# Projections of Q, K and V as three products of rounded parts; a descriptor ring of half the size, at most three scatters under way, and x normalised behind them

## What is computed

```python
x = x + xattn(layernorm(x), ctx)          # 16 heads of 16
x = x + ffn(layernorm(x))                 # 8 experts, the best 2 per token

def xattn(x_q, x_kv):
    q = split_heads(x_q @ wq.T + bq)
    k = split_heads(x_kv @ wk.T + bk)
    v = split_heads(x_kv @ wv.T + bv)
    attn = softmax(q @ k.T / 4)
    return merge_heads(attn @ v) @ wo.T + bo

def ffn(x):
    gates = top 2 of softmax((x @ Wg + bg) / 5), made to sum to 1
    return sum over experts e of gates[e] * (gelu(x @ W1[e] + b1[e]) @ W2[e] + b2[e])
```

## Time and profile before

| | us |
|---|---|
| runs: median of 3 (lowest to highest) | 797.72 (795.2 to 801.35) |
| the profiled execution's own time | 804.22 |
| its span, first to last instruction | 802.5 |
| TensorE busy | 754.3 |
| VectorE busy | 610.5 |
| ScalarE busy | 455.4 |
| GpSimd busy | 393.8 |
| attention part, from 41 (first transposed scores) to about 525 | 484 |
| tail | about 275 |

### The profile page before, as it was taken

The page is one execution under the profiler, slowest core; times in us unless marked ns, Lnnn a source line. Parts: engine busy times, 40 slices in busy tenths (PEclk is TensorE's granted clock), DMA queues, the critical chain, the costliest instruction groups (busy, mean ns, idle before and its releaser), DMA issues.

```text
span 802.5 us, 16338 instructions
## 1 busy us (share of the span) xinstructions
PE 754.3 (94%) x4672; PEld 451.0 (56%) x4672; DVE 610.5 (76%) x1127; ACT 455.4 (57%) x663; POOL 393.8 (49%) x357
## 2 busy tenths in 40 slices
PE   9999999999999999999999897869999999999995
PEld 4443344444444444444444333349999888988994
DVE  6787678798797788788788787657777887676774
ACT  2066676776766766766676674944345434443441
POOL 6506143647637728728725613306643564444444
PEclk9999999999999999999999999999999999999998
DMA  7765767657666766657658467767554465354441
GB/s 225 208 180 174 211 180 214 215 185 246 206 194 231 215 195 242 193 188 247 188 172 270 148 175 264 257 241 164 92 101 75 82 144 101 64 80 70 69 75 12
DMA packets 90660, 136.24 MB, mean 170 GB/s; under 512 B 15456, under 2 KB 49216, under 8 KB 90192
## 3 DMA queue, kind: packets, MB, share of 16 engines
q1 hardware_dynamic: 76592, 117.33, 48.4%
q0 software_dynamic: 13296, 17.09, 12.2%
q10 hardware_dynamic: 688, 0.79, 0.3%
...
## 4 chain that ended last, share of the span: by engine, by line
PE 68%; DMA 10%; issue 6%; DVE 5%; ACT 5%; SPq 4%; POOLq 1%; another core or an unknown queue 0%; POOL 0%; DVEq 0%
PE ps_pv L1576 13%; PE ring L1563 10%; PE ring L1742 8%; PE ring L1724 7%; PE ring L1550 7%; PE ps_x L1607 7%; DMA out<-y_sb,xs 7%; PE ps_x L1627 4%; ACT probs L1045 3%; PE ps_x L1617 3%; DMA den<-oT 3%; PE ring L1733 2%; DVE negm L1117 2%; PE ps_x L1637 2%; PE ps_x L1594 1%
## 5 line engine op out<-in xcount | busy, mean ns | idle before, releaser
L1117 DVE TENSOR_REDUCE negm<-ring 128x2 f32<-128x1024 f32 x256 | 310.0, 1222 | 74.3 <-PE ring L1550 63.2
L1045 ACT ACTIVATE probs<-ring 128x1024 f32<-128x1024 f32 x256 | 260.1, 1024 | 90.4 <-PE ring L1563 72.0
L926 POOL DMA_INDIRECT out<-y_sb,xs x70 | 108.8, 1554 | 152.7 <-DMA out<-y_sb,xs 81.0
L1576 PE MATMUL ps_pv<-probs,v_aug 128*32 128x512 f32 x1024 | 136.4, 605 | 3.8 <-ACT probs L1045 3.5
L1563 PE MATMUL ring<-kq 64*128 64x512 f32 x512 | 125.0, 489 | 8.1 <-DVE negm L1117 7.0
L1550 PE MATMUL ring<-kq 64*128 64x512 f32 x512 | 106.2, 413 | 9.5 <-ACT probs L1045 5.7
L1563 PEld LDWEIGHTS ring<-kq 64*128 64x128 f32 x512 | 47.3, 183 | 108.8 <-issue 73.3
L1078 ACT CAST xsT_hi<-ps_pv 128x256 fp32r<-128x256 f32 x70 | 26.1, 373 | 132.8 <-PE ps_pv L1715 120.3
L1742 PE MATMUL ring<-w_hi,hT_hi 128*128 x284 | 85.3, 300 | 0.8 <-DMA w_hi<-w_dram 0.8
L819 POOL DMA_INDIRECT xs_dram<-xg,rows x64 | 63.2, 987 | 39.5 <-issue 15.7
L1742 PE MATMUL ring<-w_lo,hT_hi 128*128 x284 | 80.2, 282 | 0.0
...
## 6 DMA issues: line engine op xcount, KB each, us to landing
...
```

The lines of the kernel that those rows point to most:

```text
L926: pool.indirect_dma_start(out=out, out_offset=bass.IndirectOffsetOnAxis(ap=xs[j % AHEAD][:, TOKEN:TOKEN + 1].bitcast(I32), axis=0), in_=re ...
L1045: nc.scalar.activation(probs[kt][:, 2 * jp:2 * jp + 2, :], ring[PLACE["ST", u, p] % RINGS][:], ACT.Exp).then_inc(exp_done, 1)
L1117: nc.vector.tensor_reduce(negm[:, v % 2, :, jp, kt], ring[PLACE["MX", v, p] % RINGS][:], AX.X, ALU.max, negate=True).then_inc(max_free, 1)
L1576: mm = nc.tensor.matmul(ps_pv[2 * DH * j:2 * DH * (j + 1), :], v_aug[:, kt, HPG * g + j, :], probs[kt][:, j, :], start=(kt == 0), stop=(kt ...
```

## The change

From batch 1 on the projections are made of three float32r products in place of one float32 product. For this the weights are split once, in the prologue: ScalarE makes `wk_hi`, `wq_hi`, `wv_hi` (128x512 each), GpSimd the low parts (`low_weights`). The context is split for each batch: ScalarE makes `kv_hi` in two halves (`high_kv`, slots (3, 3) and (3, 4)), GpSimd `kv_lo` (`low_kv`, 128x1024). Of the transposed x ScalarE makes the high part, where it made a plain copy before, and VectorE the low part (`low_x`, 128x512, slots (2, 7) and (3, 2)); `ps_x` is free only after the low part. XT0 moves from slot (2, 7) to (2, 6). The second staging of an expert's weights on ScalarE moves from (3, 2) to (3, 5).

The low parts lie where the whole values lay, and `xn_hi` where `xn` lay. So there is one `kvT` in place of two, its load waits for V1 of the batch before and stands after `fetch_o(i, 0)` and `load_w1(i)` in SyncE's order, and the normalisation of batch i+2 waits for Q1 of batch i+1.

The descriptor ring has 8192 bytes of a partition in place of the default of 16384. A scatter waits until the one three before it has landed; for this `scattered` is three semaphores. On GpSimd the scatters stand ahead of the normalisation of x and of the first low part of weights. The semaphores of b1 and b2, and of two constants, are merged; these are not shown.

```diff
-NEXT = {(2, 7): "XT0", (3, 1): "XT1"}
+NEXT = {(2, 6): "XT0", (3, 1): "XT1"}
...
+XT_LOW = {(2, 7): "XT0", (3, 2): "XT1"}
+KV_HIGH = {(3, 3): 0, (3, 4): 1}
...
+UNDER_WAY = 3
...
-STAGE_SLOTS = {(1, 2): 0, (3, 2): 1}
+STAGE_SLOTS = {(1, 2): 0, (3, 5): 1}
...
+            with ExitStack() as whole:
+                xn = whole.enter_context(nc.sbuf_tensor("xn", [P, NT, D], F32))
+                xnT = whole.enter_context(nc.sbuf_tensor("xnT", [P, DC, S], F32))
+                kvT = whole.enter_context(nc.sbuf_tensor("kvT", [P, DC, S], F32))
+                wq_sb = whole.enter_context(nc.sbuf_tensor("wq_sb", [P, DC, D], F32))
+                wk_sb = whole.enter_context(nc.sbuf_tensor("wk_sb", [P, DC, D], F32))
+                wv_sb = whole.enter_context(nc.sbuf_tensor("wv_sb", [P, DC, D], F32))
+            xn_hi = att("xn_hi", [P, NT, D], F32R)
+            xn_lo = att("xn_lo", [P, DC, S], F32R)
+            kv_lo = att("kv_lo", [P, DC, S], F32R)
+            wq_lo = att("wq_lo", [P, DC, D], F32R)
+            wk_lo = att("wk_lo", [P, DC, D], F32R)
+            wv_lo = att("wv_lo", [P, DC, D], F32R)
+            kv_hi = att("kv_hi", [P, DC, S], F32R)
...
+        def wait_scattered(eng, b):
+            for n in range(UNDER_WAY):
+                eng.wait_ge(scattered[n], 16 * len(range(n, TOPK * NT * b, UNDER_WAY)))
...
             def load_kv(b):
-                if b > 1:
-                    sp.wait_ge(full["V1"], b - 1)
-                sp.dma_start(kvT[:, b % 2], ctx_kv[b]).then_inc(kv_in, 16)
+                sp.wait_ge(full["V1"], b)
+                sp.dma_start(kvT[:], ctx_kv[b]).then_inc(kv_in, 16)
...
-                if i + 2 < B:
-                    load_kv(i + 2)
...
                     load_w1(E - 2)
+                if i + 2 < B:
+                    load_kv(i + 2)
                 if more:
...
-            load_kv(1)
             store_parts("Q", 0, 1)
             store_parts("K", 0, 1)
+            load_kv(1)
...
-            def scatter_tile(k, t):
+            def scatter_tile(b, k, t):
+                n = NT * (TOPK * b + k) + t
+                if n >= UNDER_WAY:
+                    pool.wait_ge(scattered[n % UNDER_WAY], 16 * (n // UNDER_WAY))
                 pool.indirect_dma_start(out=xs_dram, out_offset=bass.IndirectOffsetOnAxis(ap=rows[:, k, t:t + 1], axis=0),
-                                        in_=xg[:, t, :], in_offset=None).then_inc(scattered, 16)
+                                        in_=xg[:, t, :], in_offset=None).then_inc(scattered[n % UNDER_WAY], 16)
...
-                pool.wait_ge(full["XT1"], b)
+                if b == 1:
+                    pool.wait_ge(full["XT1"], b)
+                else:
+                    pool.wait_ge(full["Q1"], b)
...
+            def low_weights(n):
+                kind = "KQV"[n]
+                whole_w, high, low = w_parts[kind]
+                pool.wait_ge(full[{"K": "K1a", "Q": "Q1", "V": "V1"}[kind]], 1)
+                if kind == "V":
+                    pool.wait_ge(full["V0"], 1)
+                pool.wait_ge(w_split, 3)
+                nc.gpsimd.tensor_tensor(low[:], whole_w[:], high[:].bitcast(F32), ALU.subtract).then_inc(w_split, 1)
+            def low_kv(b):
+                pool.wait_ge(kv_split, 3 * b - 1)
+                nc.gpsimd.tensor_tensor(kv_lo[:], kvT[:], kv_hi[:].bitcast(F32), ALU.subtract).then_inc(kv_split, 1)
...
                     split("Q", i + 1, 0)
+                    split("Q", i + 1, 1)
+                    split("K", i + 1, 1)
+                if i > 1:
+                    scatter(i - 2, NP * (NG * i + 1) + SCATTER if i < B - 1 else None)
                 if i + 2 < B:
                     ln(i + 2)
-                if i + 1 < B:
-                    split("Q", i + 1, 1)
-                    split("K", i + 1, 1)
+                if i > 0:
+                    ln2(i - 1)
                 if i in STAGED:
                     low_staged(i, 0)
-                if i > 1:
-                    scatter(i - 2, NP * (NG * i + 1) + SCATTER if i < B - 1 else None)
-                if i > 0:
-                    ln2(i - 1)
-                if i + 2 < B:
-                    add_bo(i + 2)
                 if i + 1 < B:
                     for g in range(3):
                         place_v(i + 1, g)
+                if i + 2 < B:
+                    low_kv(i + 2)
+                    add_bo(i + 2)
                 if i in STAGED:
                     low_staged(i, 1)
             ln(1)
             for g in range(NG):
                 place_v(0, g)
+            for n in range(3):
+                low_weights(n)
+            low_kv(1)
...
-                if kind == "XT":
-                    if b > 0:
-                        act.wait_ge(full["Q1"], b)
+                if kind == "XT" and b == 0:
                     nc.scalar.copy(xnT[:, int(name[2]), :], ps[:]).then_inc(done[name], 1)
+                elif kind == "XT":
+                    nc.scalar.copy(xn_high(int(name[2])), ps[:].rearrange("p (t s) -> p t s", s=P)).then_inc(xt_high, 1)
...
+            def high_kv(b, c):
+                act.wait_ge(kv_in, 16 * (b + 1))
+                nc.scalar.copy(kv_hi[:, c, :], kvT[:, c, :]).then_inc(kv_split, 1)
...
+            for kind in "KQV":
+                whole_w, high, _ = w_parts[kind]
+                nc.scalar.copy(high[:], whole_w[:]).then_inc(w_split, 1)
             misc("MT", 0)
+            for c in range(DC):
+                high_kv(1, c)
             for i in range(B):
...
+            def low_x(name, b):
+                c = int(name[2])
+                dve.wait_ge(xt_high, 2 * (b - 1) + c + 1)
+                dve.wait_ge(full["Q1"], b)
+                nc.vector.tensor_tensor(xn_lo[:, c, :].rearrange("p (t s) -> p t s", s=P), ps_x[:].rearrange("p (t s) -> p t s", s=P),
+                                        xn_high(c).bitcast(F32), ALU.subtract).then_inc(done[name], 1)
...
+                    if b == 0:
+                        for c in range(DC):
+                            mm = nc.tensor.matmul(ps[:, half], w[:, c, f * P:(f + 1) * P], act_t[:, c, half],
+                                                  start=(c == 0), stop=(c == DC - 1))
+                    else:
+                        pe.wait_ge(w_split, 4 if name[0] == "K" else 5)
+                        _, w_hi, w_lo = w_parts[name[0]]
+                        for c in range(DC):
+                            if name[0] == "Q":
+                                high = xn_high(c)[:, half.start // P:half.stop // P, :]
+                                low = xn_lo[:, c, half].rearrange("p (t s) -> p t s", s=P)
+                                res = ps[:, half].rearrange("p (t s) -> p t s", s=P)
+                            else:
+                                high, low, res = kv_hi[:, c, half], kv_lo[:, c, half], ps[:, half]
+                            for n, (w, src) in enumerate(((w_hi, high), (w_hi, low), (w_lo, high))):
+                                mm = nc.tensor.matmul(res, w[:, c, f * P:(f + 1) * P], src, start=(c == 0 and n == 0),
...
+                        else:
+                            terms = [(x, w, c) for c in range(DC) for x, w in ((kv_hi, wv_hi), (kv_hi, wv_lo), (kv_lo, wv_hi))]
+                            for k, (x, w, c) in enumerate(terms):
+                                mm = nc.tensor.matmul(ps[:, h * D:(h + 1) * D], x[:, c, tokens], w[:, c, :],
+                                                      start=(k == 0), stop=(k == len(terms) - 1))
...
-    nc = bacc.Bacc("TRN2", target_bir_lowering=False, num_devices=1)
+    nc = bacc.Bacc("TRN2", target_bir_lowering=False, num_devices=1, dynamic_dma_scratch_size=8192)
```

83 lines of the change are left out of this document (47 added, 36 removed).

## The result

The changed kernel took 810.29 us (median of 4 runs, 806.51 to 812.75) beside 798.04 for the kernel before (4 runs): ratio 1.0172, 95% interval 1.0139 to 1.0205. It is slower by 12 to 14 us; the forecast was 790.3, range 775 to 799. Two later measurements on other chips (e10, e13) gave ratios of 1.0018 and 1.0040. The changed kernel took nearly the same there (808.32 and 810.13); it is the kernel before that took 807 and 805. Of the losses in the attention part, those in batch 0 and in most later batches are there too; the one ahead of batch 0 is under 1 us in place of 6.

What follows compares the result with a forecast made beforehand. TensorE was taken as the bound, VectorE right behind for a batch's first 25 us. Gains of 1.2 (batch 0), 2.3 (batch 1), 2.5 (batches 2 to 5) and 1.4 (batch 6) summed to 7.4 us: 797.7 to 790.3, range 775 to 799.

Steps and rivals of the forecast that it cites:

- What TensorE sheds: K, Q and V units on TensorE: 2.32 us for K and Q plus 0.82 for V, 3.14 us a batch.
- the rival with loads not hidden: TensorE's weight loads: 189 ns paid before each product, a batch some 9 us longer, 861 in all; chance 0.02.
- What VectorE lets through: K and Q stretch: of 2.32 us shed, 1.8 pass in batches 2 to 6, all in batch 1, 1.15 in batch 0.
- the 0.82 that I gave back: VectorE's row numbers: the split of Q1 runs earlier and misses them, so one operation falls from 1.01 to 0.19 us.
- V passes whole: V units, where VectorE waits: all 0.82 us that TensorE sheds there pass into the batch time.
- the third, 0.5 for the casts of the context: Late in a batch: casts in (3, 3) to (3, 5) hold the scores of (3, 6) and (3, 7) by 0.5 us.
- What moves on GpSimd: Batch ends: five GpSimd operations in a row make one VectorE operation wait 1.2 us in batches 1 to 5, between 0 and 2.4.
- The rival in which VectorE eats the gain: Batch ends: both VectorE operations wait for GpSimd, 6.0 us more lost, 1.4 us won, 796.3; chance 0.17.
- XT0 doesn't wait for xn: Group 2 to 3: GpSimd has xn ready at 331.0, XT0 asks at about 330.9; no cover, no wait.
- The ring and the cap: Scatters: no change taken, stops of all engines stay; ends all five gone (-4.3 us) and twice as many (+4.3).
- The slower rival: Half-size ring: twice the stops, 4.3 us in attention and 18.7 in the tail, 813; chance 0.08.
- this sign: The tail: the prediction is wrong if the tail changes by over 1 us, its instructions being the same.

Runs made afterwards that it cites:

- e10: The changed kernel once more, unchanged, on the chip of e9 and e11: 808.32 us, ratio 1.0018 to the kernel before.
- e13: The changed kernel once more, unchanged, on the chip of e15: 810.13 us, ratio 1.0040 to the kernel before.
- e2: The changed kernel with GpSimd's bias (add_bo) put ahead of kv_lo: ratio 1.0126.
- e8: e5 with VectorE's statistics of the first normalisation moved from slots (0, 3), (0, 5), (0, 6) to (1, 6), (1, 7), (2, 1): ratio 0.9955.
- e4: The kernel before with only the descriptor ring cut to 8192 bytes: ratio 0.9964.
- e5: The changed kernel with the context load ahead of the experts' weights, GpSimd's bias and second low part of weights moved, and the latter's cast at (3, 2): ratio 1.0055.
- e9: The changed kernel with the context load earlier, e8's late statistics, and ScalarE's weight stagings and GpSimd's low parts and bias reordered: 792.93 us, ratio 0.9836.
- e11: The kernel before with the 8192-byte descriptor ring again, more rounds, on the chip of e9 and e10: ratio 0.9968.
- e15: The kernel of e9 measured again, unchanged, on another chip: ratio 0.9837.

## Why the prediction was wrong

- **What TensorE sheds.** The mechanism was right: the loads stay hidden, Q's cut operand costs nothing (0.23 us a product, as whole rows), and the rival with loads not hidden is out. The term was mis-sized: 1.9 us a batch, not 3.14. I took the pace of products inside a long run from the tail; a unit between other work pays 0.1 to 0.2 more, and there are nine of them.
- **What VectorE lets through.** This step failed. I let 1.8 of 2.32 us pass in K and Q. In group 0 nothing passed: 16.44 against 15.83, and still 15.85 without the logits' stall (e2). The idle time of 0.54 and 0.46 that I counted stood ahead of slot (0, 4), and from there to (1, 4) VectorE ran with hardly a gap already, while four of the seven units are behind that point. Of the idle time itself more than half went to two operations lengthened by GpSimd's cast `qk_hi`, 0.48 and 0.52 for 0.19 each; the first of them ends with the cast:

```profile
244.77 0.61 POOL L915 CAST qk_hi<-qk 128x512 fp32r<-128x512 f32 x1 [4.04 <-ACT qk L1041]
244.95 0.48 DVE L1310 TENSOR_TENSOR oh<-sc,smax 128x32 f32<-128x32 f32 x1
```

  And the split of Q1 did not run earlier. Before it GpSimd waits for the store of Q0, and its cast and its tensor-tensor behind it, from 260.46 to 261.74, meet the row numbers:

```profile
259.76 0.61 POOL L915 CAST qk_hi<-qk 128x512 fp32r<-128x512 f32 x1 [8.19 <-DMA q_dram<-qk_lo]
259.85 0.57 DVE L1358 TENSOR_TENSOR row_k<-row_of,oh 128x32 f32<-128x32 f32 x1
...
260.68 1.11 DVE L1358 TENSOR_TENSOR row_k<-row_of,oh 128x32 f32<-128x32 f32 x1
```

  So the 0.82 that I gave back was never there. What bound group 0 is shown by e8: with 2.0 us of VectorE's statistics gone from it, it takes 14.87.
- **V passes whole.** It didn't. Group 2 is 15.32, and 15.28 in e4, which has float32 V and no stop. What V sheds goes to slot (2, 7), where the scores wait for the exponential behind XT0's cast. I had priced this wait at 0.5; it was 0.80, and XG0's was 0.26 for 0.35; the third, 0.5 for the casts of the context, doesn't appear in a steady batch:

```profile
285.60 0.49 PE L1632 MATMUL ring<-kq 64*128 64x512 f32 x2 [0.80 <-ACT probs L1109]
...
291.28 0.66 PE L1676 MATMUL ps_x<-ident,xg 128*128 128x128 f32 x4 [0.26 <-DVE xn_lo L1231]
```

- **What moves on GpSimd.** I put both VectorE operations beside the right run of GpSimd's and gave the pair 1.2 us, with 2.4 as the far end. They took 2.6. In time this cost less: 0.6 in group 0 (16.44 against 15.86 in e2) and 0.9 in group 3 (14.9 against 14.0 in e5's batch 1 and in e9), 1.5 a batch. My reason for the half, that the one that waits pushes the other into a gap, fails, since the run of three has no gap. The rival in which VectorE eats the gain describes batches 2 to 5; it ended at 796, since it still had the shed time in it. That XT0 doesn't wait for xn held, with 0.2 us to spare: xn is done at 283.1, and XT0 starts at 283.3. The Trainium skill (SBUF — State Buffer, Who interferes with whom) says that a VectorE instruction with two SBUF inputs contends with a GpSimd instruction that reads SBUF. The trace agrees for GpSimd's tensor-tensor operations, 2.67 against 0.68, and e5 and e9 take the stall away by order alone.
- **The one buffer for the context.** This step is missing, and it was the largest loss, 7 us. The diff has the load wait for V1 and puts it behind the experts' weights in SyncE's order; I named both in describing the change and priced neither. Three questions were to be asked: when is the load issued, how long does it take to land (8.2 to 12.3 us in batch 0 of the five traces with this order, behind others of 512 KB; 5.5 to 7.1 there with the load put first), and who asks for it when. That the cast asks some four slots after the issue could be counted. Behind it ScalarE's queue was the second thing to name: a cast that waits holds the exponentials.
- **The clock.** The sum has no term for TensorE at 1.2 GHz. It cost some 3 us behind the stop of 4.7, and 5 of the 6 us that the prologue lost in the first trace.
- **The ring and the cap.** The sum took the stops to stay. In the changed kernel's traces none to two are left, so a gain of some 6 us in the first pair was left out, which I had as one end, at 4.3. This is also why batch 6 seems right (forecast 1.4, measured 1.7), which is luck: 2.0 came in group 2, 1.4 of it with the stop that went (16.70 before, 15.27 in e4) and 0.6 from V, which passes there in part since no XT0 stands in batch 6 (14.67). The slower rival, 813, fell with e4 and e11, and that the time came out near it is chance. I had also called the prediction wrong if the tail changed by over 1 us. It did, by 7.5 in the first pair, but this sign was a bad one: between e13 and e15, whose tail is the same on the same chip, the experts alone differ by 3.0.

The sum, worked again with what was measured, by the traces of the first pair: prologue +6, batch 0 +7.3, batch 1 +0.4, batches 2 to 5 +0.8, +0.7, +2.5 and 0, batch 6 −1.7, in all +15.9, and −8.5 behind it: 7.4 in the spans (809.9 and 802.5). The prologue's term came by chance to this trace. Of the −8.5, 1.5 stand behind the last tile and go with the ring (e4), 1.4 stand in batch 7, and 6.0 between the first and the last first-layer product of the experts (261.6 and 255.6). The 6.0 are not explained: it is 261.5 in both traces with the full ring and 255.6 to 262.5 in those with the half.
